# Turning gathered rows by 16 SBUF transfers and 32x32 block transposes on VectorE instead of on TensorE

## The reference, cut to what matters

```python
buf = jnp.zeros((E, CAP + 1, Hq), x.dtype).at[sorted_e, dest].set(x[tok])   # E = 32, CAP = 256, Hq = 512
g = jnp.einsum('ech,ehf->ecf', buf, w_gate)                                  # F = 352
u = jnp.einsum('ech,ehf->ecf', buf, w_up)
y = jnp.einsum('ecf,efh->ech', jax.nn.silu(g) * u, w_down)
```

## Time and profile before

| | us |
|---|---|
| median of three runs | 1688.76 |
| lowest, highest | 1687.11, 1691.56 |
| the profiled execution | 1695.61 |
| its span, first to last instruction | 1693.8 |
| mean granted TensorE clock | 0.996 of full speed |

### The profile page before, as it was taken

One profiled execution on the slowest core, in us unless ns is written; L12 is line 12 of the kernel. 1 busy time (PEld: TensorE's weight loads), 2 busy tenths in 40 slices (PEclk: granted clock), 3 DMA queues, 4 the chain that ended last, 5 costly groups with the idle time before them and its releaser, 6 DMA issues.

```text
span 1693.8 us, 26093 instructions
## 1 busy us (share of the span) xinstructions
PE 1647.0 (97%) x8512; PEld 1402.2 (83%) x8512; DVE 1272.6 (75%) x1863; ACT 697.7 (41%) x1216; POOL 836.7 (49%) x691
## 2 busy tenths in 40 slices
PE   6999999998999999999998999999999999999999
PEld 4777888876999999999986788888788888888887
DVE  7989999997756555655579687676777768687776
ACT  5746555653766666666653212121221212112121
POOL 4587777774444444444457444251433525243351
PEclk9999999999999999999999999999999999999999
DMA  4544343424766666666687655454545343433431
GB/s 156 194 155 174 125 156 141 149 100 181 253 240 244 239 241 234 228 228 230 239 278 230 234 176 162 174 182 148 179 143 178 104 155 119 155 107 114 166 99 52
DMA packets 122420, 299.06 MB, mean 177 GB/s; under 512 B 19996, under 2 KB 31260, under 8 KB 117728
## 3 DMA queue, kind: packets, MB, share of 16 engines
q1 hardware_dynamic: 103104, 263.82, 43.6%
q0 software_dynamic: 18944, 33.66, 6.9%
q10 hardware_dynamic: 288, 0.52, 0.1%
HBM read 233.34 MB, written 81.35 MB: 186 GB/s over the span
## 4 chain that ended last, share of the span: by engine, by line
PE 74%; DVE 15%; issue 6%; ACT 2%; POOL 2%; another core or an unknown queue 0%; DMA 0%; DVEq 0%; POOLq 0%; ACTq 0%; SPq 0%
PE bank L2176 25%; PE bank L1400 16%; PE bank L2190 13%; PE bank L1427 8%; PE bank L2207 5%; PE bank L1024 4%; DVE mixf L719 3%; PE bank L1392 2%; DVE bank L687 1%; DVE st L667 1%; DVE mix L726 1%; DVE zT_lo L694 1%; DVE s_wg L2027 1%; PE bank L958 1%; DVE sr L740 1%
## 5 line engine op out<-in xcount | busy, mean ns | idle before, releaser
L1024 PE MATMUL bank<-mix,w 128*128 128x512 f32 x1488 | 353.7, 394 | 12.8 <-DVE ekv L735 7.6
L1024 PEld LDWEIGHTS bank<-mix,w 128*128 128x128 f32 x1488 | 277.0, 189 | 76.3 <-DVE ekv L735 5.8
L2176 PE MATMUL bank<-s_zT,s_wu 128*128 128x512 f32 x1056 | 256.7, 392 | 9.9 <-DVE bank L1932 9.9
L2190 PE MATMUL bank<-s_wd,s_h 128*128 128x512 f32 x1056 | 254.0, 390 | 1.1 <-DVE s_h L1938 1.1
L2176 PE MATMUL bank<-s_zT,s_wg 128*128 128x512 f32 x1056 | 253.7, 389 | 0.0
L2176 PEld LDWEIGHTS bank<-s_zT,s_wu 128*128 128x128 f32 x1056 | 199.5, 189 | 53.4 <-issue 11.9
L2190 PEld LDWEIGHTS bank<-s_wd,s_h 128*128 128x128 f32 x1056 | 198.4, 188 | 42.9 <-DVE s_h L1938 1.7
L2176 PEld LDWEIGHTS bank<-s_zT,s_wg 128*128 128x128 f32 x1056 | 198.2, 188 | 41.1
L1210 POOL TENSOR_TENSOR e_wg<-e_g_in,e_wg 128x1408 fp32r<-128x1408 f32 x31 | 100.7, 3249 | 212.6 <-ACT e_wg L1234 212.6
L1707 POOL DMA_INDIRECT s_picked<-y_rows,s_slot x128 | 140.6, 1099 | 78.3 <-DVE s_total L1988 39.1
L1816 ACT ACTIVATE s_act_g<-bank 128x512 f32<-128x512 f32 x88 | 52.5, 597 | 288.6 <-PE bank L2176 282.2
(11 more groups left out here) (188 smaller groups left out, 2489.3 us busy)
## 6 DMA issues: line engine op xcount, KB each, us to landing
s_wu<-wu_split SPq DMA_DIRECT2D x77, 512.0 KB
e_g_in<-in_w_gate SPq DMA_DIRECT2D x32, 704.0 KB
e_u_in<-in_w_up SPq DMA_DIRECT2D x32, 704.0 KB
e_d_in<-in_w_down SPq DMA_DIRECT2D x32, 512.0 KB
y_rows<-e_y SPq DMA_DIRECT2D x32, 512.0 KB, 2.9
s_zT<-zT_parts SPq DMA_DIRECT2D x16, 1024.0 KB, 6.8
zT_parts<-zT_hi SPq DMA_DIRECT2D x8, 1024.0 KB
zT_parts<-zT_lo SPq DMA_DIRECT2D x8, 1024.0 KB
```

Of the source, the lines that this page charges most:

```text
L1024: last = pe.matmul(pj[m][:], w[i][:, w_part, k, m * P:(m + 1) * P], mix[:, i % 2, k, x_part, :], start=(k == 0 and q == 0), stop=(k == KC ...
L2176: last = pe.matmul(into[:], w[:, w_part, k, :], zT[:, x_part, k, :], start=(q == 0 and k == 0), stop=(q == 2 and k == KC - 1))
L2190: last = pe.matmul(yp[j][:], h[:, i, h_part, j * P:(j + 1) * P], wd[f][:, w_part, :], start=(f == 0 and q == 0), stop=(f == NFS - 1 and q ...
```

## The change

For the experts 1 to 31 the transposes on TensorE go. In their place:

- SP issues 16 transfers from `rows[half]` to a new tile `apart`, once the gather has landed and the expert before has been turned (`part`). Transfer (q, a) takes the 32 partitions of quarter q, both row tiles and the 128 channels of group a, and writes them to the 32 partitions of quarter a: 64 runs of 512 bytes, 32 KB. On SP's queue the 16 stand between load(e+2) and the store of y(e), with the waits ahead of them. Those of expert 1 stand ahead of everything else that SP does in the expert stage, behind the last store of the stage before.
- VectorE issues two block transposes (`turn`), each of 128 x 512 elements in 16 blocks of 32x32, read from `apart` with a step of 4 elements and written to PSUM bank 4 or 5. On VectorE's order they stand between hidden_lo(0) and hidden(1), and wait for all 16 transfers of their expert.
- POOL's gather waits for the transfers out of `rows[half]` instead of for the turn.

Expert 0 is turned on TensorE as before.

```diff
--- before.py
+++ after.py
@@ -1113,6 +1113,7 @@
     u_in = [at("e_u_in0", [P, KC * F], 161), at("e_u_in1", [P, KC * F], 75)]
     d_in = [at("e_d_in0", [P, NF, C], 172), at("e_d_in1", [P, NF, C], 258)]
     rows = [at("e_rows0", [P, NCT, C], 184), at("e_rows1", [P, NCT, C], 56)]
+    apart = at("e_apart", [P, 2 * KC, P], 86)
     xT = [at("e_xT0", [P, 2, KC, CAP], 192, F32R), at("e_xT1", [P, 2, KC, CAP], 292, F32R)]
     act_g = at("e_act_g", [P, NF, CAP], 208)
     h = at("e_h", [P, NF, 2, CAP], 214, F32R)
@@ -1126,7 +1127,7 @@
     g_loaded, u_loaded, d_loaded = ([sem(f"e_{n}_loaded{i}") for i in range(2)] for n in "gud")
     index_made = sem("e_index_made")
     gathered = [sem(f"e_gathered{i}") for i in range(2)]
-    turned = sem("e_turned")
+    turned, parted = sem("e_turned"), sem("e_parted")
     x_hi, x_lo = sem("e_x_hi"), sem("e_x_lo")
     wg_hi, wu_hi, wd_hi = sem("e_wg_hi"), sem("e_wu_hi"), sem("e_wd_hi")
     wg_lo, wu_lo, wd_lo = sem("e_wg_lo"), sem("e_wu_lo"), sem("e_wd_lo")
@@ -1136,6 +1137,9 @@
     y_stored = [sem(f"e_y_stored{i}") for i in range(2)]
 
     shared.update(e_y_done=y_done, e_y_made=y_made, e_y_stored=y_stored, e_wg_lo=wg_lo, e_wu_lo=wu_lo, e_wd_lo=wd_lo)
+
+    Q = P // 4
+    PARTS = 16 * 16
 
     def experts(eng, one_expert):
 
@@ -1160,9 +1164,19 @@
             sp.dma_start(d_in[half][:, 0:NF - 1, :], d["w_down_a"](e)).then_inc(d_loaded[half], 16)
             sp.dma_start(d_in[half][0:FT[-1][1], NF - 1, :], d["w_down_b"](e)).then_inc(d_loaded[half], 16)
 
+        def part(e, half, uses):
+
+            sp.wait_ge(turned, e)
+            sp.wait_ge(gathered[half], uses * 32)
+            for q in range(4):
+                for a in range(4):
+                    sp.dma_start(apart[a * Q:(a + 1) * Q, q:q + 4 * NCT - 3:4, :],
+                                 rows[half][q * Q:(q + 1) * Q, :, a * P:(a + 1) * P]).then_inc(parted, 16)
+
         def one_expert(e, half, more, uses):
             if more == 2:
                 load(e + 2, half)
+                part(e + 2, half, uses + 1)
             else:
                 output_early[more]()
             sp.wait_ge(y_made, (e + 1) * NCT)
@@ -1188,6 +1202,7 @@
 
         def main(*early):
             output_early.extend(early)
+            part(1, 1, 1)
             experts(sp, one_expert)
 
         output_early = []
@@ -1195,7 +1210,9 @@
 
     def gpsimd(pool):
         def gather(e, half):
-            wait(pool, turned, e - 1)
+            wait(pool, parted, (e - 2) * PARTS)
+            if isinstance(e, int) and e == 2:
+                pool.wait_ge(turned, 1)
             wait_apart(pool, (table_loaded, 16), index_made, e + 1)
             for c in range(NCT):
                 pool.indirect_dma_start(
@@ -1326,6 +1343,16 @@
             dve.tensor_tensor(wd[half][0:m, 1, NF - 1, :], d_in[half][0:m, NF - 1, :],
                               wd[half][0:m, 0, NF - 1, :].bitcast(F32), ALU.subtract).then_inc(wd_lo, 1)
 
+        def turn(e):
+
+            dve.wait_ge(parted, e * PARTS)
+            dve.wait_ge(x_lo, e * KC)
+            for i in range(2):
+                last = dve.transpose(
+                    xt[i][:].rearrange("p (k g t) -> p k g t", k=2, t=Q),
+                    apart[:].rearrange("p g (j k) -> p k g j", k=KC)[:, 2 * i:2 * i + 2])
+            last.then_inc(turned, 1)
+
         def rows_lo(e, half):
             for k in range(KC):
                 dve.wait_ge(x_hi, e * KC + k // 2 * 2 + 2)
@@ -1353,6 +1380,8 @@
             else:
                 output_early[0]()
             hidden_lo(e, 0)
+            if more:
+                turn(e + 1)
             hidden(e, 1)
             if not more:
                 output_early[1]()
@@ -1384,9 +1413,8 @@
         return first_index, first_weights, lambda: rows_lo(0, 0), main
 
     def tensor(pe):
-        def turn(e, half, uses):
-            pe.wait_ge(gathered[half], uses * 32)
-            wait(pe, x_lo, e * KC)
+        def turn_first(half):
+            pe.wait_ge(gathered[half], 32)
             for c in range(NCT):
                 for k in range(KC):
                     last = pe.transpose(xt[k // 2][:, (k % 2) * CAP + c * P:(k % 2) * CAP + (c + 1) * P],
@@ -1432,11 +1460,9 @@
         def one_expert(e, half, more, uses):
             for f in range(NF):
                 up_gate(e, half, f)
-            if more:
-                turn(e + 1, 1 - half, uses + half)
             down(e, half)
 
-        return lambda: turn(0, 0, 1), lambda: experts(pe, one_expert)
+        return lambda: turn_first(0), lambda: experts(pe, one_expert)
 
     return sync, gpsimd, scalar, vector, tensor
```

## The result

| | us |
|---|---|
| before, median of 4 runs (lowest, highest) | 1687.93 (1686.82, 1691.56) |
| changed, median of 4 runs (lowest, highest) | 1819.19 (1816.62, 1821.06) |
| changed / before | 1.0773, 95% interval 1.0751 to 1.0794 |
| span of the profiled execution, changed | 1814.8 |

The change costs 131 us. The forecast of 1703.5 had the sign, but it held 15 of the 131 us, and its range ended at 1738.

The account below looks back on a forecast made before the run. TensorE bounds the expert stage; moving its transposes makes late transfers and VectorE's chain the bound. 30 periods at +0.35 us plus 4.3 us of start give +14.8 us, 1703.5 us carried to the median; range 1678 to 1738.

Parts of the forecast that it names:

- the likeliest case: Expert stage: transfers land late, VectorE waits, period 13.97 us, 0.35 above the period before; 1703.5 us, chance 0.42.
- all three terms of the landing: Transfers on SP's queue: gathered rows at 12.2 us, issues 7.05, last landing 2.2; sum 21.45, 22.05 with 0.6 for backlog.
- D: Time of VectorE's two block transposes per expert: 1.28 us claimed, upper bound 3.98.
- Issue ... at 0.47 are 7.05 us: SP's queue: 15 issues ahead of the last at 0.47 us each; 0.6 us more for issues slowed by queued-up data.
- SP has the time: SP's queue per expert: 16 issues take 7.5 us and its five present issues 3.1 us, so they fit.
- The rival in which SP's queue takes over: All 16 issues at 0.79 us take 11.85 us, period 16.07, 1767 us; half at that pace, 1732; chance 0.16.
- That is 12.2: Gathered rows land 12.2 us into the expert: 11.3, plus 0.6 for late ScalarE, plus 0.3 for loads beside the gather.
- The loads: no cost: Weight loads issued behind the 16 transfers are needed two periods on and land 3 us before that, costing nothing.
- the rival of the slow transposes: VectorE's strided transposes run at twice the time: D 2.56 us, period 14.6, 1723 us; chance 0.15.
- Its clock unchanged: TensorE would idle some 1.3 us an expert before the next expert's first weight load, without its clock changing.
- TensorE's 0.95 us: Removing the eight transposes from TensorE saves 0.95 us an expert in 31 experts, at most 29.5 us.
- the chain of 11.94 + D: VectorE and ScalarE chain sets the least period: 7.34 us before the transposes, D, then 4.6 to the next expert.

Follow-up runs that it names:

- the transfers alone: Kernel before, still turning on TensorE, with the 16 transfers added on SP's queue and their output read by nobody: 1752.2 us, ratio 1.039.
- The runs with the gather first: Changed kernel with POOL's gather issued ahead of the gate's subtraction: 1795.3 us; with that subtraction also behind up's, 1757.0; with two buffers as well, 1743.7.
- the two runs with turns alone: Changed kernel with only expert 1's transfers: 1717.1 us; the same with transposes reading elements side by side, blocks in wrong order: 1692.7 us.
- keeping TensorE busy: Changed kernel with seven unread fp32 matmuls on TensorE ahead of the down product in half of the experts: 1808.9 us, ratio 1.071.
- the last kernel: Changed kernel with gather three experts ahead, transposes ahead of hidden(0), 12 transfers, and four blocks copied by ScalarE: 1666.7 us, repeated at 1665.5, ratio 0.985.
- the run at 1757: Changed kernel with POOL's gather ahead of the gate's subtraction, and that subtraction waiting for up's subtraction and hidden_lo(0) on VectorE: 1757.0 us, ratio 1.041.
- 12 transfers: Changed kernel in its own order with 12 of the 16 transfers, blocks staying on their own partitions not moved: 1777.0 us, ratio 1.051.

## Why the prediction was wrong

The sign was right, and the likeliest case was a loss through transfers that come late, which is what happened. The size failed: all three terms of the landing were too small, and so were D and the tail behind it.

**The formula** held: period = (landing + D + tail) / 2, with the tail from the transposes' end to the next expert. The ring runs from the start of a short expert over the gather and the transfers to the transposes in the long one. The timelines give, as means of 14 rings, in us:

| | forecast | changed kernel |
|---|---|---|
| expert's start to gathered rows there | 12.2 | 14.5 |
| 15 issues, with what slows them | 7.65 | 9.6 |
| last issue to transposes | 2.2 | 2.8 |
| D | 1.28 | 2.04 |
| tail | 4.6 | 6.1 |
| sum, for two periods | 27.9 | 35.1 |
| period | 13.97 | 17.5 |

17.55 was measured, in two unequal parts. The ring shown above, one of the 14, runs from 662.20 to 697.41.

**"Issue ... at 0.47 are 7.05 us"** measured 9.6. In the loop each issue is 0.60 us and a gap of 0.04, in every kernel: most runs of 16 take 10.2 us, and some 10.4 to 11.8. I took the pace of four loads for transfers of another shape (32 partitions, two strided pieces each), and made the backlog the reason for slow issues. Inside the loop it is nearly a fixed price; only the very first 16, behind the last store of the stage before, take 12.2 us (0.76 each; 11.0 to 12.2 in the other kernels). With the 0.6 us that I had for the backlog this is 2.0 us of landing, 1.0 us of period.

**"SP has the time"** failed with it: 10.2 + 3.3 for y and the loads, with gaps, is 13.8 to 14.4, above 13.62. I had the sum of the issues, 7.5 + 3.1, and with their real price it no longer fits. The run with 16 transfers and the gather a stage ahead shows this bound by itself, 14.1 us and 1710; with the transfers alone (1752) the gather's wait comes on top. The rival in which SP's queue takes over had the mechanism, at 0.79 per issue instead of 0.64, and its 1767 was the nearest of my numbers; it had 0.16.

**"That is 12.2"**, the gather's landing, measured 14.5: 2.3 us of landing, 1.2 us of period. The gather is issued as early as before, 5.6 us behind the expert's start, so the 0.6 us for a late ScalarE did not come. But SP goes on 9.0 us after that issue, where the data had been there in some 5.5 (658.18 to 663.7). I had written 0.3 us for loads beside the gather, with a bound of 1.4; it was 3.5. Late issues push the loads onto the gather, and the gather makes the issues later. The runs with the gather first show it: the landing falls from 7.1 to 3.7 us, and with the subtraction out of the way 1819 becomes 1757. "The loads: no cost" failed by the same.

**"My value is 1.28"**, D, measured 2.1, inside the bounds. It is the rival of the slow transposes, at 1.56 times the pace of side by side reads instead of twice: 0.4 us of the period here, but 0.8 us of the chain where no transfer is late (the 24 us between the two runs with turns alone).

**"Its clock unchanged"** failed. A pause of 6.5 us is followed by 12 matmuls at the lower level, 1.2 GHz (5.49 against 3.04 us). It is in the tail: 6.1 us instead of 4.5, which keeping TensorE busy gave back. That is 0.7 us of period; 10 us of the whole came back, since the short experts grew.

**One uniform period** was assumed. Two experts share the rows' buffers and the ring spans two periods, so it can split into some 21.4 and 13.7, and the idle clock then adds to the longer one. The split as such I did not forecast, and why it settles in that pattern was not tried.

**Start**: 4.3 forecast, about 11 measured. Expert 1 starts 22.6 us behind the last store of SP (428.61 to 451.20), 11.8 before (436.34 to 448.13). The 16 issues take 12.16 us there, not 7.5, and the down product comes back at a granted clock of 0.50:

```profile
429.11 12.16 SPq L1173 DMA_DIRECT2D e_apart<-e_rows  x16
442.60 2.04 DVE L1351 STREAM_TRANSPOSE bank<-e_apart 128x512 f32<-128x512 f32 x2 [6.96 <-DMA e_apart<-e_rows]
...
445.91 5.49 PE L1455 MATMUL bank<-e_wd,e_h 128*128 128x512 f32 x12 [8.50 <-DVE e_h L1371]
```

**The sum as measured.** Per period 17.55 - 13.62 = 3.93; 30 x 3.93 + 11 = 129 of 131 us. By runs: turns and start 30 us (1717); 16 issues with an early gather about 40 more (1757); the late gather, with the pauses and the clock that come of it, 62 more (1819). These steps are not independent: the run at 1757 also has the shorter subtraction on VectorE.

**What was right**: TensorE's 0.95 us, shown as gain in the last kernel; the chain of 11.94 + D, 14.0 by D = 2.1 against 14.3 measured; the small packets, nearly. From 450 to 850 us SP's queue takes 54.7% of the 16 engines for 23 experts, 9.5 us each, where it had taken 54.0% for 29, 7.4 us each: 2.1 us for the 1024 packets, 32 ns each, where I had 2.9. With 16 transfers, where SP waited for no gather, the DMA share was 0.79, so the engines had room. What the packets add to the landing of other transfers was not separated.

## What to carry to other kernels

Price a DMA on the queue that issues it: instructions times their pace for that shape, plus all else in the round, and hold the sum against the period before looking at bytes. A move that adds a dependence should be followed around the whole ring, two buffers and two periods long, with the gather and the loads that it pushes into each other. Where a swap of engines shows no gain, try the order and the count first: 12 issues instead of 16, a gather one stage earlier and transposes in free time turned +7.7% into -1.5%. Issuing part of the transfers from a second queue was not tried.

## What the runs showed of the hardware

- A transfer within SBUF of 32 partitions by two pieces of 512 B costs the queue that issues it 0.64 us: 10.2 us for most runs of 16, 10.4 to 11.8 for some, and 11.0 to 12.2 for the first, behind the last store of the stage before.
- STREAM_TRANSPOSE of 128x512 fp32 into a bank: 0.70 us from elements side by side, 1.09 us with a step of 16 bytes.
- A VectorE subtraction with two SBUF inputs (128x1408) takes 1.62 us alone, also beside the issue of a gather on POOL. Beside a POOL subtraction it makes no headway and ends 1.5 us behind POOL's end: 2.50 us with 1.02 of overlap, 5.29 with 3.24.
- The gather lands 3.7 us after its issue (median) when it goes ahead of the loads, 7.1 us beside them.
- After pauses of 6.5 and 8.5 us, 12 matmuls of 128x512 took 5.49 us at a granted clock of 0.50; after one of 1.82 us (12 transfers) 4.27, in a stretch at 0.68; after one of 0.92 us 3.04, at 1.00.
